# Product keys: the mark of the best key moved to GpSimd and ScalarE, and the top eight left out by a masked product

## The reference

```
x_norm = rms(layernorm(x)) * norm_w
q   = (x_norm @ wq)                       # 8 heads, 2 halves of 128
sim = q . keys                            # 2 x 8 x 32 per token
s1, i1 = top_k(sim[0], 16); s2, i2 = top_k(sim[1], 16)
all_scores = s1[:, None] + s2[None, :]    # 256 sums per head
final_scores, pk = top_k(all_scores, 16)  # the 16 best pairs of keys
hidden = gelu(x_norm . expert_down[idx]) * relu(final_scores)
out    = sum(hidden * expert_up[idx])     # over 8 heads x 16 experts
x = x + 0.5 * out
```

## Time and profile before

| | |
|---|---|
| median of three runs | 2576.18 us |
| profiled execution | 2572.97 us, its span 2571.1 us |
| granted clock of TensorE, mean | 0.902 |
| busy over the whole span | PE 2054.2 us (80%), DVE 1767.1 (69%), ACT 1268.5 (49%), POOL 1183.5 (46%) |
| masks, L711 | 256, 1277 ns each |
| product keys, first pass | masks from 46.9 us on, last addition to x at 348.8 |
| product keys, second pass | up to 898.4 us |

### The profile page before, as it was taken

The page is one execution under the profiler, slowest core; times in us unless marked ns, Lnnn a source line. Parts: engine busy times, 40 slices in busy tenths (PEclk is TensorE's granted clock), DMA queues, the critical chain, the costliest instruction groups (busy, mean ns, idle before and its releaser), DMA issues. The chain is left out here.

```text
span 2571.1 us, 40071 instructions
## 1 busy us (share of the span) xinstructions
PE 2054.2 (80%) x11750; PEld 1625.8 (63%) x11775; DVE 1767.1 (69%) x4619; ACT 1268.5 (49%) x2385; POOL 1183.5 (46%) x1051
## 2 busy tenths in 40 slices
PE   4788869967888769966995998886992669999755
PEld 3666646645666657845774875665781458888634
DVE  5999944458999775666667556666566657887575
ACT  3666646646666554533444443334441157777321
POOL 3776740005767644521544553002550468887003
PEclk9999979988999979976997998997996879999877
DMA  1000000000000010000001000000000000000000
GB/s 54 1 0 0 1 15 1 0 0 1 0 0 0 1 54 1 0 4 1 1 0 53 1 0 26 1 0 9 1 0 0 0 10 3 6 6 0 18 0 17
DMA packets 16184, 18.40 MB, mean 7 GB/s; under 512 B 2208, under 2 KB 14048, under 8 KB 16096
## 3 DMA queue, kind: packets, MB, share of 16 engines
q1 hardware_dynamic: 16096, 17.35, 2.2%
HBM read 16.30 MB, written 1.05 MB: 7 GB/s over the span
## 5 line engine op out<-in xcount | busy, mean ns | idle before, releaser
L1107 POOL TENSOR_TENSOR unit_hid_low<-unit_hid,unit_hid_high 128x512 fp32r<-128x512 f32 x272 | 351.4, 1292 | 378.1 <-ACT unit_hid_high L1084 378.1
L711 DVE SCALAR_TENSOR_TENSOR pk_chosen<-bank,pk_least,pk_sums 128x1024 f32<-128x1024 f32 x256 | 325.1, 1277 | 37.1 <-ACT pk_sums L609 19.4
L609 ACT COPY pk_sums<-bank 128x1024 f32<-128x1024 f32 x256 | 258.8, 1015 | 176.7 <-PE bank L495 171.0
L495 PE MATMUL bank<-pk_pick,pk_sim_both 128*128 128x512 f32 x512 | 193.9, 462 | 107.6 <-DVE pk_chosen L711 106.7
L1031 PE MATMUL bank<-unit_x_high,units_high 128*128 x544 | 220.8, 406 | 13.3 <-PEq L832 8.2
L414 POOL TENSOR_TENSOR pk_chosen<-pk_chosen 128x1024 f32<-128x1024 f32 x96 | 226.7, 2375 | 7.6 <-DVE pk_chosen L711 7.6
L1032 PE MATMUL bank<-unit_x_low,units_high 128*128 x544 | 217.5, 400 | 0.0
L1033 PE MATMUL bank<-unit_x_high,units_low 128*128 x544 | 217.1, 399 | 0.0
L495 PEld LDWEIGHTS bank<-pk_pick,pk_sim_both 128*128 128x128 f32 x512 | 80.5, 197 | 163.5 <-DVE pk_chosen L711 153.5
L1077 ACT ACTIVATE unit_gact<-bank,units_small 128x512 f32<-128x512 f32 x136 | 93.6, 688 | 169.0 <-PE bank L1034 169.0
L1117 DVE SCALAR_TENSOR_TENSOR unit_prod<-bank,units_small,unit_gact 128x512 f32<-128x512 f32 x136 | 102.1, 751 | 105.9 <-ACT unit_gact L1077 105.8
(11 more groups left out here) (374 smaller groups left out, 5159.2 us busy)
## 6 DMA issues: line engine op xcount, KB each, us to landing
raw<-in_geglu_units SPq DMA_DIRECT2D x3, 774.0 KB, 6.4
raw<-in_swiglu_units SPq DMA_DIRECT2D x3, 768.0 KB, 6.7
dh_w_next<-in_de_w SPq DMA_DIRECT2D x8, 192.0 KB, 2.3
out_x<-x_res SPq DMA_DIRECT2D x1, 1024.0 KB, 5.1
raw<-in_geglu_units SPq DMA_DIRECT2D x1, 967.5 KB, 9.9
raw<-in_swiglu_units SPq DMA_DIRECT2D x1, 960.0 KB, 10.6
pk_down<-in_pk_downT SPq DMA_DIRECT2D x1, 512.0 KB, 5.3
pk_up<-in_pk_up SPq DMA_DIRECT2D x1, 512.0 KB, 6.5
```

The lines of the kernel that those rows point to most:

```text
L495: ins = nc.tensor.matmul(sums_ps[:, 2 * b + e, :], both[:, odd, h, :], pk.pick[:, e * PK_K // 2:(e + 1) * PK_K // 2, :].rearrange("p i j - ...
L609: nc.scalar.copy(sums_sb[:, b, :].rearrange("p (e n) -> p e n", e=2), sums_ps[:, 2 * b:2 * b + 2, :]).then_inc(sums_out.sem, 1)
L711: nc.vector.scalar_tensor_tensor(chosen[:, h, :].rearrange("p (e n) -> p e n", e=2), sums_ps[:, 2 * b:2 * b + 2, :], least2[:, odd, h:h + ...
L1107: nc.gpsimd.tensor_tensor(hid_low[:, i % HB, :], hid[:, i % HB, :], hid_high[:, i % HB, :].bitcast(FP32), ALU.subtract).then_inc(hidden.se ...
```

## The change

1. The mark of the best key. VectorE's comparison (L679) goes. GpSimd subtracts all scores of the second half from the best one (`pk_below`: 0 at the best key, above 0 elsewhere), ahead of its other sums, and tells ScalarE by a new counter; ScalarE takes the sign of that in `tell_others`, behind `read_added`, which gives `not_best`. GpSimd waits for it ahead of its last product, as it waited for VectorE.
2. The top eight. Instead of a match-and-replace per head, one instruction per head: where a candidate is less than the eighth best (`top[:, h, 7:8]`) it is multiplied by 1, elsewhere by 0. Both tensor operands of this instruction are the same tile, `cand`, in SBUF.

```
--- before.py
+++ after.py
...
@@ -358,6 +358,7 @@
         parts = k.scratch(ctx, "pk_sim_parts", [P, PK_H, 2, 2 * PK_K], FP32R)
         both = k.scratch(ctx, "pk_sim_both", [P, 2, PK_H, P], FP32R)
         best = k.scratch(ctx, "pk_best", [P, PK_H, 2, PK_BEST])
+        below = k.scratch(ctx, "pk_below", [P, PK_H, PK_K])
         not_best = k.scratch(ctx, "pk_not_best", [P, PK_H, PK_K])
         cand = k.scratch(ctx, "pk_cand", [P, PK_H, PK_CAND])
         cand_rest = k.scratch(ctx, "pk_cand_rest", [P, PK_H, PK_CAND])
@@ -392,6 +393,8 @@
                 sims = sims2[:, odd]
 
                 pool.wait_ge(best_ready.sem, best_ready.at(i + 1))
+                nc.gpsimd.tensor_tensor(below[:], best[:, :, 1, 0:1].to_broadcast([P, PK_H, PK_K]), sims[:, :, 1, :],
+                                        ALU.subtract).then_inc(below_ready.sem, 1)
                 nc.gpsimd.tensor_tensor(cand[:, :, 0:PK_K], sims[:, :, 0, :],
                                         best[:, :, 1, 0:1].to_broadcast([P, PK_H, PK_K]), ALU.add)
                 nc.gpsimd.tensor_tensor(cand[:, :, PK_K:2 * PK_K], sims[:, :, 1, :],
@@ -591,6 +594,11 @@
                 nc.scalar.copy(sims2[:, odd].rearrange("p h a k -> p (h a k)"), high_ps).then_inc(sim_out.sem, 1)
                 nc.scalar.copy(parts[:, :, 0, :], high_ps.rearrange("p (h n) -> p h n", h=PK_H)).then_inc(sim_high.sem, 1)
 
+            def tell_others(i):
+
+                act.wait_ge(below_ready.sem, below_ready.at(i + 1))
+                nc.scalar.activation(not_best[:], below[:], ACT.Sign).then_inc(second.sem, 1)
+
             def read_turned(i, odd, e):
 
                 act.wait_ge(sim_t.sem, sim_t.at(2 * i + e + 1))
@@ -635,6 +643,8 @@
                             read_turned(i + 1, 1 - odd, 1)
                         if not first:
                             read_added(i - 1)
+                        if not last:
+                            tell_others(i + 1)
                     if h == 3:
                         read_hidden(i, odd, 0)
                     if h == 4:
@@ -646,6 +656,7 @@
             read_turned(0, 0, 0)
             read_turned(0, 0, 1)
             read_sims(1, 1)
+            tell_others(0)
             read_sums(0, 0)
             read_sums(0, 1)
             period(0, 0, first=True)
@@ -674,12 +685,6 @@
                 if PK_H - 1 in heads:
                     ins.then_inc(best_ready.sem, 1)
 
-            def find_not_best(i, odd):
-                nc.vector.drain()
-                nc.vector.tensor_tensor(not_best[:], sims2[:, odd, :, 1, :],
-                                        best[:, :, 1, 0:1].to_broadcast([P, PK_H, PK_K]),
-                                        ALU.not_equal).then_inc(second.sem, 1)
-
             def find_top(i, heads):
                 if 0 in heads:
 
@@ -691,7 +696,8 @@
 
             def leave_top_out(heads):
                 for h in heads:
-                    nc.vector.match_replace(cand_rest[:, h, :], top[:, h, 0:8], cand[:, h, :], NEG)
+                    nc.vector.scalar_tensor_tensor(cand_rest[:, h, :], cand[:, h, :], top[:, h, 7:8], cand[:, h, :],
+                                                   op0=ALU.is_lt, op1=ALU.mult)
 
             def find_rest(odd):
                 nc.vector.drain()
@@ -722,7 +728,6 @@
                         find_best(i + 1, 1 - odd, LOWER)
                     if h == 1:
                         find_best(i + 1, 1 - odd, UPPER)
-                        find_not_best(i + 1, 1 - odd)
                     if h == 3:
                         find_top(i + 1, LOWER)
                     if h == 4:
@@ -736,7 +741,6 @@
 
             find_best(0, 0, LOWER)
             find_best(0, 0, UPPER)
-            find_not_best(0, 0)
             find_top(0, range(PK_H))
             leave_top_out(LOWER)
             leave_top_out(UPPER)
...
```

More of the change, by code:

```diff
@@ L37 @@
 STAGE_COUNTERS = ("""
-    pk_tile_in pk_sim pk_sim_out pk_sim_t pk_sim_t_out pk_sim_high pk_sim_low pk_best pk_second pk_cand
+    pk_tile_in pk_sim pk_sim_out pk_sim_t pk_sim_t_out pk_sim_high pk_sim_low pk_best pk_below pk_second pk_cand
     pk_sums pk_sums_out pk_masked pk_paired pk_combined pk_added_out pk_hidden pk_gelu pk_weighted
@@ L347, in product_key_ffn @@
     names = ("pk_tile_in", "pk_sim", "pk_sim_out", "pk_sim_high", "pk_sim_low", "pk_sim_t", "pk_sim_t_out", "pk_best",
-             "pk_second", "pk_cand", "pk_sums", "pk_sums_out", "pk_masked", "pk_paired", "pk_combined", "pk_added_out",
+             "pk_below", "pk_second", "pk_cand", "pk_sums", "pk_sums_out", "pk_masked", "pk_paired", "pk_combined", "pk_added_out",
              "pk_hidden", "pk_gelu", "pk_weighted", "pk_product", "pk_product_out")
-    (tile_in, sim, sim_out, sim_high, sim_low, sim_t, sim_t_out, best_ready, second, cand_ready, sums, sums_out, masked,
+    (tile_in, sim, sim_out, sim_high, sim_low, sim_t, sim_t_out, best_ready, below_ready, second, cand_ready, sums, sums_out, masked,
      paired, combined, added_out, hidden, gelu, weighted, product, product_out) = [k.counter(n) for n in names]
@@ L675, in find_best @@
                     ins.then_inc(best_ready.sem, 1)
[L677 to L681, removed]
             def find_top(i, heads):
@@ L751, in _ @@
             nc.vector.tensor_tensor(k.x[:], k.x[:], halved[:], ALU.add)
-    for s in (tile_in, sim, sim_out, sim_high, sim_low, best_ready, second, cand_ready, added_out, weighted, product,
+    for s in (tile_in, sim, sim_out, sim_high, sim_low, best_ready, below_ready, second, cand_ready, added_out, weighted, product,
               product_out):
```

## The result

| | before | after |
|---|---|---|
| median | 2577.18 us (4 runs, 2570.57 to 2578.2) | 2729.16 us (4 runs, 2728.58 to 2733.64) |
| ratio to before, 95% interval | | 1.0599 (1.0578 to 1.0621) |
| profiled execution, its span | 2572.97 and 2571.1 us | 2733.64 and 2731.9 us |
| first pass, first mask to last addition to x | 301.9 us | 379.4 us |
| its granted clock | 0.97 | 0.86 |

A forecast was written before the change was run, and what follows sets the result against it. VectorE's queue was taken to bound the stage. 30 tiles by 5.9 us (177) plus 6.4 us ahead of the first tiles made 183 us, on a median of 2576.2: 2759 us, range 2660 to 2805.

The forecast's parts named there:

- Late candidates: In each tile, GpSimd's last product waits for ScalarE's sign: candidates ready at 8.0 us in place of 7.08.
- VectorE's queue as the stage's time: In the product-key stage, VectorE is fullest (268.4 of 301.9 us), so its queue sets the time.
- rival C: No waits at the port, and the mark's 0.82 us per tile are earned: 25 us, 2551 us; chance 0.04.
- Turns at the port: Behind mask h5, four products alternate with GpSimd's SBUF-reading operations: mask h6 5.9 us later per tile.
- price of a turn: At h5, each product between GpSimd operations adds 0.1 us; the last ends 0.28 behind pair 2, mask h6 at 18.25.
- The end of the tile: From mask h6 to the next tile's first mask: unchanged, 5.83 us.
- The sum: Over both passes, 30 tiles by 5.9 us make 177 us; with 6.4 us ahead of first tiles, 183 us.
- Ahead of the first tile: At each pass's start nothing hides the wait for the sign: 3.2 us, twice, 6.4 us.
- Half clock in every tile: TensorE's idling lowers its clock, ScalarE's read of the added tile comes 1.45 us later: 44 us, upper end 2803.
- GpSimd's gap ahead of the candidates: In each tile, GpSimd's idle time before the candidates was to grow; no size given.
- Rival A: VectorE's four products keep their turn, one wait per group: 2.85 us more per tile, 2667 us; chance 0.12.
- B: One tile read twice counts as one input, no port waits; only late candidates cost, 22 us: 2598 us; chance 0.08.

The follow-up runs named there:

- third experiment: Changed kernel with match-and-replace in place of the products, and the sign earlier in ScalarE's queue, ahead of the second reading of the turned scores: 2576.54 us, ratio 1.0011.
- fifth experiment: Changed kernel with GpSimd's three pair additions replaced by fills with nought, which read no large tile and leave out that adding: 2589.8 us, ratio 1.0061.
- first: Changed kernel with match-and-replace back in place of the masked products, the mark staying with GpSimd and ScalarE: 2600.23 us, ratio 1.0106.
- seventh: Kernel before with no mark of the best key at all, so the best pair counts twice: 2571.4 us, ratio 0.9984.
- v1_halves: Kernel of the third experiment, with GpSimd forming the candidates of heads 0 to 3 as soon as their best are known: 2554.61 us, ratio 0.9925.
- v3_halves_mark_vector: Kernel before, mark still on VectorE, with GpSimd forming the candidates of heads 0 to 3 early: 2570.28 us, ratio 0.9985.

## Why the prediction was right, and which term was off

Point by point, for the tile of 72.59:

- Late candidates: said 8.0, measured 7.94 (79.84 + 0.69 - 72.59), the last product 0.07 us behind the sign's end. The third experiment shows the sign's place as cause of the difference to 7.50. The rest, 7.50 against 7.08, is GpSimd's new subtraction (0.59 us from its start to the next), less 0.18 for the sum that no longer runs beside the mark; the subtraction was named but stood hidden behind the sign.
- VectorE's queue as the stage's time: this reading of the earlier trace rows did not hold. At full clock the 10.8 us of GpSimd's queue set the tile already before the change, and the last wait of each tile, L701 for `split_low`, lay inside an instruction's length, where the list of waits does not show it. The forecast did not suffer, since with the products both queues are tied together at pair 2; rival C, which earned the mark's 0.82 us, rested on it alone.
- Mask h4: the mean moved from 8.52 to 8.95, 0.4 us.
- Turns at the port: held, with the lengths said (the first at half a microsecond, two at 2.4; those at h6 0.24). Their place was right: weight, take, pair 1, pair 2.
- **The mis-sized term is the price of a turn.** The sum gave GpSimd 0.1 us for each product between two of its operations and 0.28 us behind pair 2, and mask h6 at 18.25. Measured: the two pairs take 4.65 us, no more than the 4.71 of the earlier trace rows without any product between them, and mask h6 stands 17.49 behind h0. Weight ended at 12.59 (said 12.7), pair 2 at 17.46 (said 17.97), the last product 0.11 behind it. So a waiting product costs VectorE a whole GpSimd operation and GpSimd nothing that the rows show.
- The end of the tile, from mask h6 on: said unchanged, 5.83. It is 6.34 in the mean of 14 tiles (before 5.95). L707 (0.17 us alone) ends at 96.03, `split_low` at 96.00, and the copies that `split_low` needs come from TensorE at half clock (0.50 in the window from 91.30 to 94.30), behind an idle stretch of 4.47 us (said: some 3 us):

```profile
91.41 1.22 PE L498 MATMUL bank<-pk_pick,pk_sim_both 128*128 128x512 f32 x2 [4.47 <-DVE pk_chosen L717]
```

```profile
91.30:94.30 3.00, 2.89 (x11) 2.60 (x12) 2.91 (x12) 1.64 (x3) 0.00 (x0) 0.50 0.00 0
```

- The sum: 30 tiles by 5.1 us are 153 (said 177, 5.9 each). In the 14 tiles of the table it is 5.26: mask h6 comes 0.74 earlier than said, mask h6 of before stands at 12.64 in the mean and not at the 12.34 of the one tile that the forecast started from (0.30 less), and the longer end gives 0.39 back. Ahead of the first tile 4.1 us (said 3.2; the rounding of the second tile's scores, 43.43 in the earlier trace rows, came at 44.42, 1.0 us later, ahead of any step of the change that it could wait for), between the passes 1.4, in the last tiles of the two passes 1.3 together, and 1.0 behind the second pass, in blocks that the change leaves alone. Together 160.8, the difference of the two profiled spans. The medians lie 152 us apart, since the profiled execution was the slowest of the changed kernel's four, and that of before stood below its median.

```profile
44.42 0.59 ACT L595 CAST pk_sim_parts<-bank 128x512 fp32r<-128x512 f32 x1
44.90 0.43 ACT L600 ACTIVATE pk_not_best<-pk_below 128x256 f32<-128x256 f32 x1
...
45.41 0.68 POOL L411 TENSOR_TENSOR pk_cand<-pk_cand,pk_not_best 128x256 f32<-128x256 f32 x1 [2.89 <-ACT pk_not_best L600]
```

- In the second pass the wait ahead of the first tile was as long as in the first (2.90 us), but the stretch between the passes grew by 1.4 us only: the start of the attention took 4.9 us (granted clock 0.92) where it had taken 6.9 (0.75).
- Half clock in every tile: the bound of 2803 supposed that it delays `read_added`. It came in 26 of the 30 tiles, but behind mask h6, where VectorE has work of its own; `read_added` ended 6.87 behind h0 as before, and 7.11 at the latest.
- GpSimd's gap ahead of the candidates was to grow; it did not (4.47 us, 4.48 in the earlier trace rows). VectorE's first masks run as before, and the new idle time, 4.68 us, stands ahead of `split_low`.
- Rival A (one wait per group) falls by the single products; B (one tile read twice is one input) by those and by the fifth experiment; C (the mark is earned) by the first and seventh. C's mechanism gave at most 0.6% (v1_halves against v3_halves_mark_vector), not 1%, and only with the candidates formed earlier.

## What to carry to other kernels

Before taking work off the fullest engine, find which wait ends last in a tile, and follow it back: here that was GpSimd's queue behind the candidates, so the mark was worth nothing until they came earlier, and then 0.6% at most. Count the SBUF operands of each VectorE instruction that stands beside a GpSimd queue: a small two-input instruction waits for a whole GpSimd operation, so four of 0.24 us cost 5.4; the replaces, which read `cand` once, took 0.23 us at the same place. And a port wait shows in no list of waits: look for an instruction whose longest is many times its shortest (here 2410 and 292 ns; 761 and 171 for L701 in the kernel before).

## What the runs showed of the hardware

- VectorE and GpSimd take strict turns when both have a queue of such operations: 2.39 and 2.38 us for products of 0.24, with 2.35 and 2.34 us of GpSimd's. In the changed kernel the third product of four took over 1 us in 28 of 32 groups. The same tile as both operands counts as two inputs.
- The waiting side pays all: GpSimd's two pairs took 4.65 us with a product between them and 4.71 without. The other way round it is GpSimd that pays: its second sum took 0.81 us beside VectorE's mark and 0.63 in the kernel without one.
- A small one-input instruction, L707, 128x8, waits for a GpSimd operation too: 0.17 us ahead of the first tile, 1.14 us beside `split_low`, with its end 0.03 us behind it. In the kernel before L701 did the same (0.74 us, ending 0.02 us behind `split_low`), and the forecast's 5.83 us took it for fixed. With all eight products behind mask h6, where `split_low` had long ended, it took 0.17 us in every tile. The Trainium skill (SBUF — State Buffer, Who interferes with whom) lets instructions in a two-port mode contend as well; whether L707 runs in one, no row shows.
- TensorE's idle stretch has an after-price: 2.25 us idle, then pairs of matmuls of 1.15 us in place of 0.70, and a tile of 19.14 us in place of 18.41.
